# A decoder layer's attention on one core: the key-major score half moved ahead of the query-major half in each slot

## The reference

```python
def _mha(q_in, k_in, v_in, ..., mask):          # 16 heads of 8
    scores = einsum('bhqd,bhkd->bhqk', q, k) / sqrt(hd)
    if mask is not None:
        scores = where(mask == 0, -1e9, scores)
    attn = softmax(scores, axis=-1)
    return einsum('bhqk,bhkd->bhqd', attn, v) @ ow + ob   # heads put together
x = layernorm(x + _mha(x, x, x, mask))          # self-attention
x = layernorm(x + _mha(x, ctx, ctx, None))      # cross-attention
x = layernorm(x + relu(x @ w1 + b1) @ w2 + b2)
phi = elu(x); KV = elu(ctx).T @ ctx             # linear attention, per batch
x = layernorm(x + (phi @ KV) / (phi @ elu(ctx).sum() + 1e-6))
```

## Time and profile before

| | us |
|---|---|
| median of 3 runs (lowest to highest) | 297.97 (297.59 to 301.7) |
| the profiled execution | 296.94 |
| its span, first to last instruction | 295.0 |
| one iteration in the steady part (128.2 to 157.6) | 29.4 |

### The profile page before, as it was taken

How to read it: one execution, slowest core, us unless ns; L and a number is a source line. 1 busy time by engine, 2 the same in 40 slices (tenths; PEclk the granted TensorE clock), 3 DMA queues, 4 the chain that set the end, 5 groups by cost and what they waited for, 6 DMA issues and landing times.

```text
span 295.0 us, 8346 instructions
## 1 busy us (share of the span) xinstructions
PE 254.9 (86%) x3047; PEld 158.7 (54%) x3047; DVE 190.6 (65%) x601; ACT 152.8 (52%) x370; POOL 116.3 (39%) x226
## 2 busy tenths in 40 slices
PE   7959679889999999999999999999999978879860
PEld 3424334555576557655765576556655754645630
DVE  7055255678848985898589848984897555454140
ACT  3005423565657565756575757575747573364220
POOL 5020230133225363536353735372537354532835
PEclk9997856999999999999999999999999999999995
DMA  4390111311211122112211221112110001000000
GB/s 127 104 269 0 55 41 36 81 53 43 80 58 26 31 81 76 24 32 80 76 25 38 73 77 26 37 45 76 26 33 16 19 14 37 20 13 0 11 6 18
DMA packets 28623, 14.60 MB, mean 49 GB/s; under 512 B 8024, under 2 KB 28200, under 8 KB 28584
## 3 DMA queue, kind: packets, MB, share of 16 engines
q1 hardware_dynamic: 27576, 13.61, 16.2%
q10 hardware_dynamic: 1008, 0.47, 0.5%
HBM read 5.46 MB, written 1.05 MB: 22 GB/s over the span
## 4 chain that ended last, share of the span: by engine, by line
PE 63%; DVE 18%; issue 6%; SPq 5%; DMA 3%; ACT 2%; POOL 2%; POOLq 0%; DVEq 0%; ACTq 0%
PE av_ps L461 9%; PE proj_ps L491 9%; DVE neg_max L842 7%; PE s_ps L391 6%; PE proj_ps L525 6%; PE s_ps L433 5%; PE s_ps L411 5%; SPq L295 5%; PE s_ps L379 4%; PE post_ps L481 4%; PE s_ps L443 3%; PE post_ps L477 3%; DMA w_sb<-in_weights 2%; DVE att L872 2%; PE proj_ps L504 2%
## 5 line engine op out<-in xcount | busy, mean ns | idle before, releaser
L680 ACT ACTIVATE probs<-s_ps 128x512 f32<-128x512 f32 (+1 forms) x128 | 72.0, 592 | 52.8 <-PE s_ps L443 52.8
L842 DVE TENSOR_REDUCE neg_max<-s_ps 128x4 f32<-128x512 f32 (+1 forms) x128 | 68.4, 575 | 36.5 <-PE s_ps L411 36.3
L1042 POOL TENSOR_SCALAR var_e<-mv 128x1 f32<-128x1 f32 x32 | 7.2, 224 | 97.3 <-DVE mv L893 97.3
L379 PE MATMUL s_ps<-zeros_b 128*128 128x512 bf16 x115 | 29.7, 395 | 1.0 <-POOL zeros_b L1017 1.0
L443 PE MATMUL s_ps<-max_x,unit_sel 64*128 64x256 bf16 (+1 forms) x256 | 24.9, 274 | 0.0
L686 ACT COPY av_sb<-av_ps 128x256 f32<-128x256 f32 x32 | 11.7, 365 | 23.8 <-PE av_ps L461 23.8
L491 PE MATMUL proj_ps<-x_t,w_sb 128*128 128x256 f32 x80 | 22.2, 395 | 0.7 <-issue 0.6
L391 PE MATMUL s_ps<-bias_q,id_b 64*64 64x512 bf16 x128 | 14.1, 428 | 8.5 <-DVE neg_max L842 3.7
L1051 POOL TENSOR_TENSOR y_g<-y_n,row_sb 128x128 f32<-128x128 f32 x32 | 14.6, 457 | 16.5 <-DVE y_n L899 16.5
L858 DVE TENSOR_TENSOR max_x<-s_ps,max_is_j 128x256 bf16<-128x256 bf16 x32 | 13.6, 425 | 11.2 <-PE s_ps L420 11.2
L461 PE MATMUL av_ps<-probs,v_aug_s 128*32 128x128 f32 x512 | 20.6, 279 | 0.2 <-ACT probs L680 0.2
(11 more groups left out here) (110 smaller groups left out, 504.4 us busy)
## 6 DMA issues: line engine op xcount, KB each, us to landing
xt_in<-in_x_t SPq DMA_DIRECT2D x8, 128.0 KB, 2.3
sq_wide<-sq_hi SPq DMA_DIRECT2D x32, 32.0 KB, 2.3
sq_wide<-sq_lo SPq DMA_DIRECT2D x32, 32.0 KB, 1.9
x_all<-in_x SPq DMA_DIRECT2D x8, 128.0 KB, 2.4
cq_wide<-cq_hi SPq DMA_DIRECT2D x32, 32.0 KB, 1.9
cq_wide<-cq_lo SPq DMA_DIRECT2D x32, 32.0 KB, 1.9
out<-o_all SPq DMA_DIRECT2D x8, 128.0 KB, 2.0
sk_rows<-sk_hi SPq DMA_DIRECT2D x14, 64.0 KB, 1.9
```

Of the source, the lines that this page charges most:

```text
L379: nc.tensor.matmul(bank[:, :], zeros_b[:], zeros_b[:].unsqueeze(1).to_broadcast([P, RH, S]), start=True, stop=True, skip_group_check=True)
L680: nc.scalar.activation(probs[0:n, h, r, :, :, :].rearrange("p u j n -> p (u j n)"), s2_ps[r][0:n, :], ACT.Exp, scale=SCALE).then_inc(M["ex ...
L842: nc.vector.tensor_reduce(neg_max[:, b, r, RH * h:RH * (h + 1)], scores, AX_X, ALU.max, negate=True).then_inc(M["max_done"], 1)
```

## The change

In PE's program, two calls change places: key_major of the current job, half 0, stands ahead of query_major of the next job, half 0. Both halves, all their instructions and their waits are as before, and no other engine's program is touched. Both calls exist in 29 of the slots; where only one of them exists, nothing changes.

```diff
                     if prev:
                         times_v(i, *prev, 1)
                     blanks(i, k, "scores")
+                    if cur:
+                        key_major(*cur, 0)
                     if nxt:
                         query_major(*nxt, 0)
-                    if cur:
-                        key_major(*cur, 0)
                     blanks(i, k, "y")
                     light_work(i, k, 0)
                     blanks(i, k, "pv")
```

## The result

The changed kernel takes 309.41 us (median of 4 runs, 308.06 to 310.08), against 297.78 (median of 4, 297.5 to 301.7) for the kernel before: 1.035 of its time, 95% interval 1.026 to 1.045. It is slower by 11.6 us; 9.5 were forecast, the time itself at 307.0. The profiled execution has a span of 306.1 us, 11.1 more than before.

What follows compares the result with a forecast made beforehand. PE, waiting on DVE's reductions, was taken as the bound. Terms 6.85 + 0.83 + 0.54 + 1.1 + 0.2 gave 9.5 us more: 306.5 from the profiled execution, 307.5 from the median, 307.0 predicted; range 303 to 311.5, widened to 301.5 to 312.

Steps and rivals of the forecast that it cites:

- The bound and the chain: PE bounds the kernel; query-major half 0, two DVE reductions and a waiting PE instruction set the time in slots 2 and 3.
- Slot 3: Cross-attention slot: query-major half 1 already waits for the reductions, so their later start costs 0.54 us.
- Slot 2: Cross-attention slot: the reductions start 0.54 us later, x3 and L533 too; cost 0.54 us.
- Slot 0: Self-attention slot: key-major half of 0.88 us, partly hidden by a filled gap and DVE's light work; cost 0.22 us.
- Slot 1: Reductions at 136.93 against 136.62, rden at 137.71 against 137.64; cost 0.07 us, upper bound 0.31.
- Steady part in sum: Iterations 2 to 6 cost 6.85 us, iteration 7 costs 0.83, slot 2 of iteration 8 costs 0.54.
- Iteration 0: Slot 0 at half clock: 1.3 us of uncovered PE idle time, some coming back; 1.1 us taken, bounds 0.7 and 2.9.
- Iteration 1: Slot 0 gains 0.3 us by filling PE's wait on max_x, slots 1 to 3 cost 0.5 together; +0.2 us.
- The rival with the clock in every iteration: One stretch at half clock in each of iterations 2 to 7 adds 7.4 us: 314 us; chance 8%.
- so I add nothing: Steady iterations: slots 2 and 3 stay above the lowest PE density seen at full clock, so no clock cost is added.
- PEclk at 9 in every slice after the first third: Sign expected in the profile after: PE's clock digit stays at 9; 5 to 8 in the middle would be wrong.
- The cover rival: PE's later waits come from its own order, so filled gaps are left over: 3.6 us faster, 293.3 us; chance 5%.

Runs made afterwards that it cites:

- the short reductions: Kernels before and changed, each with DVE's reductions over only the last 16 keys of each head: 289.47 us in the old order, 286.11 in the new.
- after_again: The changed kernel run and profiled once more, nothing edited: 308.79 us, ratio 1.028 to the kernel before.
- early_new: The kernel before with the new order in iterations 0 and 1 only, 5 of 29 slots: 301.57 us, ratio 1.0077.
- steady_new: The kernel before with the new order from iteration 2 on, 24 of 29 slots: 307.86 us, ratio 1.027.

## Why the prediction was right, and where it was off

The mechanism was right in slots 0, 2 and 3. That the total came out so near owes something to luck: the steady part was forecast 1.6 us too high, and the early part, with the clock's scatter, came out above its value.

- **The bound and the chain** (query-major half 0, two reductions, a waiting PE instruction): right. The rows of slots 2 and 3, and above all the short reductions, show it.
- **Slot 3**, forecast 0.54: 0.57.
- **Slot 2**, forecast 0.54: 0.45. The term was mis-sized. I took the length of the cross-attention half from its start to the start of L541 behind it, 0.54. In the new order L411 stands behind it and starts 0.47 after it (in slot 3, with L391 behind it, 0.56). The length of a group of matmuls depends on which group follows. The low end of the range took 0.35 for a shortest half; no row has one so short, and the moves measured 0.47 and 0.56.
- **Slot 0**, forecast 0.22: 0.24.
- **Slot 1**, forecast +0.07: -0.14. Two steps failed. The half's length was again too long (142.65 to 143.44 is 0.79, not 0.88), which makes 0.07 into about zero; and "no row of PE waits for the exponentials in a way that matters" was wrong in this slot, where L391 of key-major half 1 had waited for one until 138.59 and started at 138.64. That was visible in the trace before.
- **Steady part in sum:** forecast 8.22, measured 6.65 by the traces.
- **Iteration 0**, forecast 1.1 with 0.7 to 2.9: 3.22 in the first profile, which is above the range. For its slot 0 the means over ten profiles differ by 1.45, and slots with an equally long stretch at half clock by 0.85 and 1.2. The step that a longer stretch at half clock could follow was a bound, not the value; the stretch scatters in the old order too, and what the order adds to its length is open.
- **Iteration 1**, forecast +0.2: 1.57 in the first profile. That is scatter too: after_again, with the same program, takes 24.85 us from the third to the seventh L420, where before takes 24.87, after 26.44 and early_new 26.97; the clock rose at 51.3 us in after_again, at 55.1 in after and at 56.6 in early_new. Iterations 0 and 1 together were forecast at 1.3 and cost 1.9 to 2.3 by the times of early_new.
- **The rival with the clock in every iteration** did not come: the page has PEclk at 9 in every slice from the eighth to the last but one, with PE idle for 0.90 us at a time. But "so I add nothing" went too far, and so did "PEclk at 9 in every slice after the first third": in after_again, the same program, the clock fell in iteration 7, and the interval concerned is 2.4 us longer. The cover rival holds in slot 1 alone, and there it does win.
- **The total** came out 2.1 us above the forecast increase in the first series. In the second, after_again against before, the same change costs 9.45 us by the medians and 8.5 by the ratio (1.028, 1.019 to 1.038). steady_new and early_new together give 8.0 and 2.3, 10.3 us. So the 11.6 is the highest of three measurements whose intervals overlap, and nothing in it calls for a further cause.

## What to carry to other kernels

In a hand-ordered software pipeline, put first what starts the longest chain on another engine, and let the work whose consumer has slack run in that chain's shadow; the price of the wrong order is the length of the piece in front, less whatever light work the other engine had to do anyway. Look at each slot by itself: here one and the same swap costs 0.57 us in one slot and gains 0.14 in another. A cheap proof of such a chain is to shorten the suspected link in both versions and to see, slot by slot, whether their difference goes: the sum alone can vanish by a balance, as it did here in part.

## What the runs showed of the hardware

The same instructions of iteration 0, behind the same wait for weights, ran at half clock for anything from 3.4 to 10.2 us in different executions, and a slot of about 10 us came out 2.65 us apart; the steady slots repeat to 0.01 or 0.02 us. Near the end the clock fell in some profiles and not in others, after_again and after among them with one program, without an idle time of PE over 0.90 us ahead of it. A difference of a few us between two single profiles should be sought in the steady part first. In iteration 4 of the kernel after, the group behind a group of four matmuls of 256 columns (L443) started 0.22 us after it where this was L411, and 0.31 us after it where it was L391; before L541, in the kernel before, it was 0.31 too.
